# Slot attention with a mixture of experts: first query sets together, another order in the attention rounds, context steps of the expert stage moved

## What is computed

```python
Pn = rmsnorm(P, input_norm_w)
k_proj = Pn @ Wk.T
v_proj = Pn @ Wv.T
for _ in range(3):
    sn = rmsnorm(slots, slot_norm_w)
    q_proj = sn @ Wq.T
    scores = jnp.einsum('bkd,bmd->bkm', q_proj, k_proj) * SCALE
    attn = jax.nn.softmax(scores, axis=-2)
    attn = attn / (jnp.sum(attn, axis=-1, keepdims=True) + EPS)
    updates = jnp.einsum('bkm,bmd->bkd', attn, v_proj)
    slots = gru_cell(updates, slots, ...)
...
x = x + attention(layernorm(x), ctx_1024, ...)
x = x + ffn(layernorm(x), router_w, w1, w2)   # top 2 of 8 experts, exact gelu
```

## Time and profile before

| what | value |
|---|---|
| median of 3 runs | 798.88 us (798.15 to 799.27) |
| profiled execution | 797.23 us, of which the span from first to last instruction is 795.4 us |
| mean granted clock of TensorE | 0.905 of full speed |
| DVE busy | 661.9 us (83%) |
| PE busy | 620.8 us (78%), weight loads 530.9 us (67%) |
| POOL busy | 522.2 us (66%) |
| ACT busy | 498.8 us (63%) |

### The profile page before, as it was taken

How to read it: one execution, slowest core, us unless ns; L and a number is a source line. 1 busy time by engine, 2 the same in 40 slices (tenths; PEclk the granted TensorE clock), 3 DMA queues, 4 the chain that set the end, 5 groups by cost and what they waited for, 6 DMA issues and landing times.

```text
span 795.4 us, 28457 instructions
## 1 busy us (share of the span) xinstructions
PE 620.8 (78%) x12300; PEld 530.9 (67%) x12300; DVE 661.9 (83%) x1382; ACT 498.8 (63%) x1000; POOL 522.2 (66%) x446
## 2 busy tenths in 40 slices
PE   2556699986677699995768699996686789998697
PEld 1445699973455589884445589996354579997475
DVE  4777799995998699996899679998699779998575
ACT  3665466664877366664878356665678546665475
POOL 5984588877666377878477178878497358788100
PEclk9767999997989799998889689999799879999799
DMA  9664100000788700000487900000197600000000
GB/s 186 163 169 142 31 3 4 4 4 12 157 158 159 169 4 4 3 4 14 112 171 149 199 13 3 4 4 2 39 209 158 132 2 4 4 3 4 0 2 13
DMA packets 89928, 52.05 MB, mean 65 GB/s; under 512 B 75907, under 2 KB 84755, under 8 KB 89803
## 3 DMA queue, kind: packets, MB, share of 16 engines
q1 hardware_dynamic: 89803, 50.23, 29.4%
HBM read 30.29 MB, written 0.92 MB: 39 GB/s over the span
## 4 chain that ended last, share of the span: by engine, by line
DVE 37%; PE 28%; issue 11%; POOL 10%; ACT 8%; DMA 5%; SPq 1%; POOLq 0%; DVEq 0%; ACTq 0%
PE upd_ps L441 5%; DVE top L979 5%; DVE soft L1010 5%; POOL ctx_raw L750 5%; PE score_ps L428 4%; DVE ctx_rows L841 4%; DVE score_ps L986 4%; PE score_ps L488 4%; PE upd_ps L446 4%; DVE ssq L837 3%; DVE inv_sum L1024 3%; DMA ctx_raw<-in_ctx_dram 3%; POOL ctx_rstd L748 3%; DVE hidden L1046 2%; PE gru_ps L406 2%
## 5 line engine op out<-in xcount | busy, mean ns | idle before, releaser
L488 PEld LDWEIGHTS score_ps<-w_t,hidden 128*128 128x128 f16 x1536 | 98.2, 102 | 94.0 <-DVE hidden L1046 81.5
L802 POOL TENSOR_TENSOR attn<-soft,attn 125x672 f16<-125x672 f32 x96 | 140.8, 1466 | 29.3 <-ACT attn L678 28.4
L488 PE MATMUL score_ps<-w_t,hidden 128*128 128x128 f16 x1536 | 113.6, 228 | 56.5 <-DVE hidden L1046 56.4
L808 POOL TENSOR_TENSOR soft<-soft,rden 125x672 f32<-125x672 f32 x96 | 126.1, 1314 | 17.8 <-DVE rden L1004 17.8
L428 PE MATMUL score_ps<-qk,ctx_cols 128*128 128x56 f16 x3456 | 113.4, 192 | 4.9 <-DVE qk L884 4.8
L428 PEld LDWEIGHTS score_ps<-qk,ctx_cols 128*128 128x128 f16 x3456 | 109.3, 99 | 5.9 <-DVE qk L884 5.3
L750 POOL TENSOR_TENSOR ctx_raw<-ctx_raw,ctx_rstd 125x1536 f32<-125x1536 f32 x32 | 109.0, 3408 | 2.5
L441 PE MATMUL upd_ps<-attn,ctx_rows 126*128 126x56 f16 x3456 | 107.9, 189 | 3.4 <-POOL attn L802 3.1
L441 PEld LDWEIGHTS upd_ps<-attn,ctx_rows 126*128 126x128 f16 x3456 | 105.3, 97 | 5.4 <-POOL attn L802 4.9
L692 ACT ACTIVATE soft<-soft 125x672 f32<-125x672 f32 x96 | 73.3, 763 | 46.0 <-DVE soft L1010 45.7
L979 DVE TENSOR_REDUCE top<-score_ps 125x12 f32<-125x672 f32 x96 | 82.0, 854 | 23.5 <-PE score_ps L428 22.5
(11 more groups left out here) (132 smaller groups left out, 1225.9 us busy)
## 6 DMA issues: line engine op xcount, KB each, us to landing
ctx_raw<-in_ctx_dram SPq DMA_DIRECT2D x32, 672.0 KB
soft<-in_L_ffn_w_dram SPq DMA_DIRECT2D x16, 256.0 KB, 5.2
ctx_raw<-in_ctx_dram SPq DMA_DIRECT2D x32, 78.0 KB
x_in<-in_x_dram SPq DMA_DIRECT2D x4, 224.0 KB, 2.8
out_dram<-acc SPq DMA_DIRECT2D x4, 224.0 KB, 3.3
ctx_cols<-ctx_rows SPq DMA_TRANSPOSE x24, 7.3
soft<-in_L_xattn_gru_wih_dram SPq DMA_DIRECT2D x1, 192.0 KB, 3.8
soft<-in_L_xattn_gru_whh_dram SPq DMA_DIRECT2D x1, 192.0 KB, 4.5
```

The costliest lines, as they stand in the source:

```text
L488: mm = pe.matmul(score_ps[:, 2 + e % 2, t * D:(t + 1) * D], hidden[:, n % HRING, hp, t * ROWS:t * ROWS + D], w2_t[:, wp, e, c * D:(c + 1) ...
L802: nc.gpsimd.tensor_tensor(attn[0:TP, s % 3, LO], soft[0:TP, s % 4], attn[0:TP, s % 3, HI], ALU.subtract).then_inc(attn_ready, 1)
L808: nc.gpsimd.tensor_tensor(a, a, rden[0:TP, s % 2].unsqueeze(2).to_broadcast([TP, CHUNKS, SLOTS]), ALU.mult).then_inc(soft_ready, 1)
```

## The change

- **Queries.** The four sets of the first iteration are made together, ahead of the attention stage (in the prologue or the FFN stage before), by wide instructions where one set was made there. `queries_at` begins with set 4, so that rounds 0, 2 and 4 make none.
- **Attention order.** On DVE the subtraction (`soft`) of a round moves ahead of `dup_ps`, and the reciprocal `rden` behind the GRU's last two instructions. As `den_ps` and `dup_ps` lie in a bank that later scores write, `scores` waits for `rden_ready`. On PE `scores` moves ahead of `turn_q`.
- **FFN stage.** `rows_hi` of batch 0 and `square_ctx` of batch 2 move from the units to the end of the drain, `rows_lo` of batch 0 behind the router's probabilities. The rest follows: `rows_hi` of batch b from unit 4b + 2 to 4b - 4, `rows_lo` from 4b + 3 to 4b - 3, `square_ctx` from 4b - 5 to 4b - 10, `sum_squares` from 4b - 4 to 4b - 6. On POOL `rstd_rows` moves behind `scale_ctx` of batch 3.

```diff
         h_rstd = sb("h_rstd", [GW, 1])
+        first_ms = sb("first_ms", [GW, NG])
+        first_rstd = sb("first_rstd", [GW, NG])
         z_gate = sb("z_gate", [128, GW])
...
             m, rest = divmod(n + 2, GROUP)
-            return m if rest == 0 and m < GSTEPS else None
+            return m if rest == 0 and NG <= m < GSTEPS else None
...
+            def first_queries(i):
+                wait(pe, h_squared, nth(i, GSTEPS, NG))
+                for m in range(NG):
+                    pe.matmul(gru_ps[0:GW, 0, m:m + 1], ycols[:, m * GW:(m + 1) * GW], ones[:, 0:1], start=True, stop=True)
+                for m in range(NG):
+                    mm = pe.matmul(gru_ps[0:GW, 1, m * D:(m + 1) * D], h[:, m, :], wqk[:, :], start=True, stop=True)
+                mm.then_inc(q_mm, NG)
+            def turn_first_q(i):
+                wait(pe, q_ready, nth(i, GSTEPS, NG))
+                for m in range(NG):
+                    mm = pe.transpose(gru_ps[:, 0, m * GW:(m + 1) * GW], normed[:, m, :], ident[0:GW, 0:GW])
+                mm.then_inc(q_turned, NG)
             def turn_q(i, m):
...
                         wait(pe, cols_turned[b], nth(i - 1, DMA, DMA))
-                wait_reuse(pe, shift_ready, i, STEPS, s - 1)
+                if s >= 3:
+                    wait(pe, rden_ready, nth(i, STEPS, s - 2))
+                else:
+                    wait_reuse(pe, shift_ready, i, STEPS, s - 1)
                 for c in range(CHUNKS):
...
                 if k == 3:
-                    queries(0, 0)
+                    first_queries(0)
                 if k == 6:
-                    turn_q(0, 0)
+                    turn_first_q(0)
...
                         update(i, n - LAG)
+                    if n + 1 < STEPS:
+                        scores(i, n + 1)
                     if m is not None:
                         turn_q(i, m)
-                    if n + 1 < STEPS:
-                        scores(i, n + 1)
                     if tile_done_at(n) is not None and tile_done_at(n) < RT - 1:
...
                 mm.then_inc(logits_ready, 1)
-                if not isinstance(i, int) or i == 0:
+                if i == 0:
                     pe.wait_ge(wtile_copied, 2 * WTILES)
...
                     if more and n == QUERIES_AT:
-                        queries(i + 1, 0)
+                        first_queries(i + 1)
                     if more and n == TURN_Q_AT:
-                        turn_q(i + 1, 0)
+                        turn_first_q(i + 1)
                 if more:
...
             def square_h(i, m):
-                if m >= NG:
-                    wait(act, h_ready, nth(i, GSTEPS, m - NG + 1))
+                wait(act, h_ready, nth(i, GSTEPS, m - NG + 1))
                 wait_reuse(act, q_mm, i, GSTEPS, m)
...
                     .then_inc(qk_hi_ready, 1)
+            def first_square_h(i):
+                nc.scalar.activation(ycols[:, :], hflat, ACT.Square).then_inc(h_squared, NG)
+            def first_sum_of_squares(i):
+                wait(act, q_mm, nth(i, GSTEPS, NG))
+                nc.scalar.activation(first_ms[:, :], gru_ps[0:GW, 0, 0:NG], ACT.Identity, bias=h_eps[:, :], scale=1.0)\
+                    .then_inc(h_ms_ready, NG)
+            def scale_first_q(i):
+                wait(act, h_rstd_ready, nth(i, GSTEPS, NG))
+                for m in range(NG):
+                    ins = nc.scalar.activation(normed[:, m, :], gru_ps[0:GW, 1, m * D:(m + 1) * D], ACT.Copy,
+                                               scale=first_rstd[:, m:m + 1])
+                ins.then_inc(q_ready, NG)
+            def first_qk_hi(i):
+                wait(act, q_turned, nth(i, GSTEPS, NG))
+                nc.scalar.activation(qk[:, :, HI, :], gru_ps[:, 0, 0:PW].rearrange("p (g w) -> p g w", g=NG), ACT.Copy,
+                                     scale=key_scale[:, :]).then_inc(qk_hi_ready, NG)
...
                 if k == 2:
-                    square_h(0, 0)
+                    wait(act, cols_ready, nth(0, LN_PER, 1))
+                    first_square_h(0)
                 if k == 3:
-                    sum_of_squares(0, 0)
+                    first_sum_of_squares(0)
                 if k == 5:
-                    scale_q(0, 0)
+                    scale_first_q(0)
                 if k == 6:
-                    qk_hi(0, 0)
+                    first_qk_hi(0)
...
                         qk_hi(i, m)
+                if more:
+                    rows_hi(i + 1, 0)
+                    square_ctx(i + 1, EARLY)
                 copy_cols(ycols[:, :], score_ps[:, 3], nth(i, LNT_PER, ln_tile(RT - 1)))
...
                     if more:
-                        if c == 3 and EARLY <= e + 2 < PAIR:
-                            square_ctx(i + 1, e + 2)
-                        if c == 2:
-                            rows_hi(i + 1, e)
+                        if c == 0 and e + 1 < PAIR:
+                            rows_hi(i + 1, e + 1)
+                        if c == 2 and e + EARLY + 1 < PAIR:
+                            square_ctx(i + 1, e + EARLY + 1)
                         if n == 4 * HC + 3:
...
                             wait(act, cols_ready, nth(i + 1, LN_PER, 1))
-                            square_h(i + 1, 0)
+                            first_square_h(i + 1)
                         if n == QUERIES_AT + 1:
-                            sum_of_squares(i + 1, 0)
+                            first_sum_of_squares(i + 1)
                         if n == TURN_Q_AT - 1:
-                            scale_q(i + 1, 0)
+                            scale_first_q(i + 1)
                         if n == TURN_Q_AT + 2:
-                            qk_hi(i + 1, 0)
+                            first_qk_hi(i + 1)
                 if more:
...
                 nc.gpsimd.tensor_tensor(h_rstd[:, :], h_ms[:, :], mhalf[0:GW, 0:1], ALU.pow).then_inc(h_rstd_ready, 1)
+            def first_rstd_h(i):
+                wait(pool, h_ms_ready, nth(i, GSTEPS, NG))
+                nc.gpsimd.tensor_tensor(first_rstd[:, :], first_ms[:, :], mhalf[0:GW, 0:NG], ALU.pow)\
+                    .then_inc(h_rstd_ready, NG)
...
                 if b == 4:
-                    rstd_h(0, 0)
+                    first_rstd_h(0)
...
                         if e == EXPERTS - 2:
-                            rstd_h(i + 1, 0)
-                        if e == 2:
+                            first_rstd_h(i + 1)
+                        if e == 3:
                             rstd_rows(nth(i + 1, LNT_PER, RT))
...
                                                op0=ALU.mult, op1=ALU.subtract).then_inc(qk_ready, 1)
+            def first_qk_lo(i):
+                wait(dve, qk_hi_ready, nth(i, GSTEPS, NG))
+                nc.vector.scalar_tensor_tensor(out=qk[:, :, LO, :],
+                                               in0=gru_ps[:, 0, 0:PW].rearrange("p (g w) -> p g w", g=NG),
+                                               scalar=key_scale[:, :], in1=qk[:, :, HI, :],
+                                               op0=ALU.mult, op1=ALU.subtract).then_inc(qk_ready, NG)
...
                 if k == 7:
-                    qk_lo(0, 0)
+                    first_qk_lo(0)
...
                             .then_inc(npre_ready, 1)
-                    if 0 <= s < STEPS:
-                        wait(dve, den_ready, nth(i, STEPS, s + 1))
-                        nc.vector.tensor_scalar(dup_ps, den_ps, 1.0 / ATTN_UP, None, ALU.mult).then_inc(den_scaled, 1)
-                        wait(dve, den_scaled, nth(i, STEPS, s + 1))
-                        wait_reuse(dve, soft_ready, i, STEPS, s - 1)
-                        nc.vector.reciprocal(rden[0:TP, s % 2], dup_ps).then_inc(rden_ready, 1)
                     if n < STEPS:
...
                                                 tops, ALU.subtract).then_inc(shift_ready, 1)
+                    if 0 <= s < STEPS:
+                        wait(dve, den_ready, nth(i, STEPS, s + 1))
+                        nc.vector.tensor_scalar(dup_ps, den_ps, 1.0 / ATTN_UP, None, ALU.mult).then_inc(den_scaled, 1)
                     if done is not None:
...
                         nc.vector.tensor_tensor(h[:, done % NG, :], zh[:, :], z_cand_home(done), ALU.subtract).then_inc(h_ready, 1)
+                    if 0 <= s < STEPS:
+                        wait(dve, den_scaled, nth(i, STEPS, s + 1))
+                        wait_reuse(dve, soft_ready, i, STEPS, s - 1)
+                        nc.vector.reciprocal(rden[0:TP, s % 2], dup_ps).then_inc(rden_ready, 1)
                     if gs is not None:
...
                 router_probs(i)
+                if more:
+                    rows_lo(i + 1, 0)
                 for n in range(CH + HC):
...
                         mix_weights()
+                    if more and c == 2 and e + EARLY < PAIR:
+                        sum_squares(i + 1, e + EARLY)
                     if e >= 1 and c == 2:
...
                     if more:
```

(8 more changed lines are left out.)

## The result

The changed kernel takes 859.99 us (median of 4 runs, 858.39 to 861.2) against 798.94 (798.15 to 799.27) for the kernel before: ratio 1.0761, 95% interval 1.0726 to 1.0795, so 61 us or 7.6% slower. Its profiled execution took 861.02 us with a span of 858.9.

What follows compares the result with a forecast made beforehand. No single engine bounds the kernel everywhere; DVE has little room in attention, and the FFN moves close a latency loop over POOL. 797.2 + 82.5 - 20 - 6 = 853.7 profiled, 855 us as median, range 836 to 875.

Steps and rivals of the forecast that it cites:

- The loop over POOL: FFN stage: ACT's `rows_hi` waits for POOL, DVE for ACT, POOL for DVE's next sum; 12.39 us a batch.
- the third rival: FFN stage: DVE's unit work holds up POOL, whose multiplication stays long, +26 us, 881 in all; chance 0.07.
- The first rival: FFN stage: `rows_hi` finds its rows ready and DVE stays the bound; 764 us in all; chance 0.05.
- the loop with a gap: FFN stage: ACT waits, but part of the loop overlaps, say 10.4 us a batch; 825 us in all; chance 0.07.
- `rden` too late: Attention rounds: POOL waits for `rden` in each second round, +22 us instead of -6; 883 in all; chance 0.06.
- the FFN term: Three FFN stages: +27.1, +27.6 and +27.8 us from the closed circle of waits through POOL, +82.5 us in all.
- some of it is beside ACT's work, I take 1.0 (0 to 2.6): FFN stage, batch 6: eight query matmuls before an `up` take 2.6 us, of which 1.0 was counted.
- the tail: End of an FFN stage, after `rows_hi` of batch 7: last seven units with nothing to wait for, 16.5 us.
- The moves into the drain cost nothing: FFN drain: ACT's 3.83 us idle before `ycols` covers `rows_hi` and `square_ctx`; without it 3 us more a stage.
- That wait goes: FFN stage: ACT's 2.91 us wait for the load of batch 3 disappears; no gain counted.
- Queries and order: Attention stages: queries ahead -20 us (-8 to -24), new order of the rounds -6 us.
- DVE's waits for scores shrink below 1 us: First attention rounds: sign expected in the profile after; before, DVE waited 1.95 and 2.85 us for scores.

Runs made afterwards that it cites:

- ffn_only: The kernel before with the FFN moves alone, without the queries ahead or the new attention order: 878.34 us, ratio 1.0976.
- distance_3: The changed kernel with `rows_hi` and `rows_lo` one unit later, three units behind the sum instead of two: 810.67 us, ratio 1.0151.
- no_ffn: The changed kernel with the FFN moves undone, keeping queries ahead and the new attention order: 781.09 us, ratio 0.9767.
- pe_order_only: The kernel before with only PE's order changed, `scores` ahead of `turn_q`: 788.88 us, ratio 0.9874.
- queries_only: The kernel before with only the four query sets of the first iteration made together ahead: 791.69 us, ratio 0.9893.

## Why the prediction was right or wrong

**The loop over POOL: right in mechanism and in size.** The prediction had 12.39 us a batch; it is 12.38, and from the sum of batch 2 to its `rows_hi` it is 7.26 in all three stages, as forecast. `rows_hi` to DVE's low half is 2.39 (2.40 predicted), on to the sum 2.74 (2.73), and from the sum to the next `rows_hi` 7.25 (7.26). (The 0.04 from POOL to ACT was read at a row that had waited for DVE; from POOL's end at 220.72 to `rows_hi` at 220.76 it is the same.) ACT waits 95.4 us for POOL in these stages and 97.8 in all, somewhat over the 80 to 90 of the prediction. The multiplication takes 2.75 in all 18 passes (median over the kernel 2.753, before 3.034), so the third rival fell; this is what the rule of the Trainium skill (SBUF — State Buffer, "Who interferes with whom") gave for a POOL read without a DVE instruction of two SBUF inputs beside it. The first rival (DVE stays the bound) and the loop with a gap fell with the 12.38, and `rden` too late with the shorter attention stages. `ffn_only` and `distance_3` make the cause shown, not only argued: the moves alone cost it, and one unit more between sum and rows gives a shorter loop.

**The sum of the FFN term: 4 us too small** (+86.7 against +82.5). The step that was mis-sized is "some of it is beside ACT's work, I take 1.0 (0 to 2.6)", for the four query sets in the loop of batch 6. They cost 15.50 - 12.38 = 3.1. PE's and ACT's timelines there:

```profile
259.90 1.66 PE L415 MATMUL gru_ps<-ones,ycols 128*112 128x1 f32 x8 [5.04 <-ACT ycols L650]
...
261.42 2.03 PE L417 MATMUL gru_ps<-wqk,h 128*112 128x128 f32 x8
...
263.24 1.33 PE L496 MATMUL upd_ps<-ycols,w_t 128*128 128x448 f16 x3
...
264.61 0.53 ACT L754 ACTIVATE upd_ps<-upd_ps 128x448 f32<-128x448 f32 x1 [3.86 <-PE upd_ps L496]
```

All 16 matmuls stand ahead of an `up` that ACT waits for, and they begin after 5 us in which PE was idle: they take 3.34 us from the first to that `up`, and nearly all of it is on the path. In `no_ffn`, without the loop, they take 1.75 (234.64 to 236.39). The 2.6 for the eight of L417 was not too low, they took 2.03; but the eight of L415 were left out, and next to nothing was beside ACT's work. In three stages that is 6.4 us more than taken. Two things took 2.2 of it back. The two windows that made the later stages 0.5 and 0.7 us shorter before ended 0.5 and 0.6 us ahead of the next `top`; the three stages were equal, so 1.2 us of the sum was not there. And the tail, predicted 16.5, was 16.9, 15.5 and 16.2 (from the `rows_hi` of batch 7 at 273.40, 480.97 and 687.83 to the next `top`).

**The moves into the drain cost nothing: right.** The squares of batch 2 end at 187.76 and `ycols` begins at 188.81 after a wait for PE, so the cover held. "That wait goes" was wrong: ACT waits 3.30 us for the load of batch 3 at 200.09. It was off the path, as POOL was late next in any case: the sum of batch 2 did not wait for it, and `rows_hi` waited 5.02 us for POOL at 208.38. Over the kernel 19.3 us of such waits remain, 12.1 of them in the FFN stages, before 13.7 there.

**Queries and order: -26 predicted, -26.5 measured, and wrong in each part.** The prediction gave 20 to the queries and 6 to the order; the runs give 15.5 and 21.8, each by itself, and 25.8 together. That the sum came out right is luck. Two steps failed. The gain of 6 for the order ("`rden` comes later by `soft`'s 0.80 us", "in odd rounds by more") looked at DVE's row of instructions only; it left out that the new order also takes `turn_q` from before `scores` on PE. That alone is worth 10 us (`pe_order_only`), and it removes the wait that I had booked to the queries. And the steady rounds gain 0.18 us each, 2.9 in the 16 rounds behind the head and 11.5 in four stages, where 6 was taken out of a most of 14; both halves of the order are needed for it. "DVE's waits for scores shrink below 1 us" was wrong as well. DVE's timeline in the second attention stage, against the earlier trace rows:

```profile
302.78 0.86 DVE L1035 TENSOR_REDUCE top<-score_ps 125x12 f32<-125x672 f32 x1 [2.82 <-PE score_ps L449]
```

Two waits have become one, of 2.82 us. What is late next is what the prediction named, the first update over POOL's work, but it was not priced as a wait of DVE. PE's timeline, where the scores for that `top` stand behind the update:

```profile
294.94 1.09 PE L449 MATMUL score_ps<-qk,ctx_cols 128*128 128x56 f16 x36 [1.71 <-DVE rden L1078]
298.57 1.37 PE L462 MATMUL upd_ps<-attn,ctx_rows 126*128 126x56 f16 x36 [2.54 <-POOL attn L851]
...
300.88 1.86 PE L449 MATMUL score_ps<-qk,ctx_cols 128*128 128x56 f16 x36
```

The wait of `scores` on `rden_ready` (1.71 us, once a stage) made no `top` late, so its price of nothing was right.

**Prologue and side costs: too low.** The wide queries cost 3.4 us in the prologue, where 0 (0 to 3) was taken. ACT waited 2.75 us there for L417, whose eight took 2.03; but in `no_ffn` they took 1.11 and the prologue was still 2.7 us longer than before, so their slowness is not most of it, and what is stays open. In the FFN stages they cost 3 us of `no_ffn` and 7 of `queries_only`; which wait makes up that difference was not followed.

The sum in one line: FFN +4.2, prologue +3.4, attention -0.5 make 7.1 us; the profiled execution took 861.0, 7.3 more than the 853.7 that were forecast.

## What to carry to other kernels

With in-order engines, count for every producer the units to its consumer, then look what is queued behind the waiting consumer: if the producer of the next item is reached only through it, the latency round the circle is the period, however idle the engines are. Moving one step of such a circle earlier shortens the distance of another, and opening one circle can uncover a second one, here over the load slots, so write down all of them before moving anything. And a wait that two edits can remove is won once: price each edit alone and both together, on the engine where the wait starts, not only where it shows.

## What the runs showed of the hardware

- The same eight L415 and eight L417 matmuls took 1.66 and 2.03 us behind 5.04 us of idle time on PE, and 0.95 and 1.11 in `no_ffn` without it, 1.75 and 1.83 times as long. The granted clock was 0.50 from 259.9 to 263.3, the lower of the two levels (1.2 GHz), and 1.00 (2.4 GHz) from 234.6 to 236.4 in `no_ffn`. Over a whole stage it was 0.78 to 0.83, before 0.90 to 0.91. Here the idle time that the circle made was paid a second time, in the matmuls behind it on the path.
- In a closed circle POOL's power over 125x12 counts in full: 2.27 us, where an addition of the same shape took 0.21.
- POOL's multiplication over 125x1536 had a median of 2.75 us after and 3.03 before, and the mean of `rows_lo` on DVE went from 2.29 to 1.87 us. That the two meet more rarely in the idle stage would explain both; no run measured it by itself.
